# Two large transfers in place of eight small ones for the shifted copy of V in a local-attention layer

## The chip, the cores and the metric

The kernel runs on one core of a Trainium2 chip. The metric is device time in microseconds (us) of one execution. TensorE (PE in the rows) multiplies matrices, VectorE (DVE), ScalarE (ACT) and GpSimd (POOL) do the elementwise work, and SyncE (SP) issues the transfers, which 16 DMA engines carry out. Each engine works through its own list of instructions in order, and semaphores tie the lists together.

## The reference

A tensor of 2 x 1024 tokens with 128 channels goes through eight residual stages. Most of the time goes into a stage that comes twice, a stack of six layers with local attention. Cut to what matters here:

```python
def local_attention(q, k, v):              # 16 heads of 64, windows of w = 32 tokens
    bq, bk, bv = (t.reshape(b, h, n // w, w, d) for t in (q, k, v))
    def look(t):                           # the window before, and the window itself
        p = jnp.pad(t, ((0, 0), (0, 0), (1, 0), (0, 0), (0, 0)))
        return jnp.concatenate([p[:, :, :nw], p[:, :, 1:]], axis=3)
    bk2, bv2 = look(bk), look(bv)
    sim = jnp.einsum('bhwie,bhwje->bhwij', bq, bk2) * QK_SCALE
    ...
    attn = jax.nn.softmax(sim, -1)
    return jnp.einsum('bhwij,bhwje->bhwie', attn, bv2)

for i in range(DEPTH):                     # DEPTH = 6
    x = attn_layer(shift_tokens(x), Wqkv[i], q_scale[i], k_scale[i], Wo[i]) + x
    x = ffn_layer(shift_tokens(x), ln_g[i], ln_b[i], W1[i], b1[i], W2[i], b2[i]) + x
```

So each query looks at the 32 tokens of its own window and at the 32 before them.

## The kernel before

`window_layers` computes the six layers, and is called twice. Its work is cut into positions `(l, b, p)`: layer, batch, and pair of heads (8 pairs). Each engine has a function `position`, which writes out that engine's instructions of one position; layer 0 and the tail are written out, layers 1 to 5 are a hardware loop. In position `p`, a pair's queries and keys are made, while the scores, the maximum, the softmax and the values (`values`, L1470, and the sums of the weights, L1475) of the pair before, `p - 1`, are computed.

V is made for four heads, that is for two pairs, at once, in four tiles V0 to V3 of two 128-token units each (products L1530, evictions by ScalarE at L1685 into the tile `V[j % 2]`, 128 x 8 x 256 floats). The last of the four is made in an even position; in an odd one, the values begin to use it. Tokens lie on partitions, 128 to a unit, so that half of the 64 keys of a query block lie at another partition offset than V has them. For these there is a second tile, `V_early`, the same values 32 tokens later: partitions 32 to 127 hold V's partitions 0 to 95, and partitions 0 to 31 hold V's 96 to 127 of the unit before. The SP queue makes it by transfers from SBUF to SBUF (`shift`, L1315). `values` reads `V_early` and `V` in turn; in odd positions it first waits for the semaphore `v_moved`.

In an even position SP works in this order: `w_qk`'s load, when GpSimd has split the weights before them (`wqk_split`); `w_v`'s load (L1310), when GpSimd has split the `w_v` before (`wv_split`, whose second half is L1745); then the copies into `V_early`. Ahead of them stand a wait for the values that last read that buffer (`pv_full`) and waits for V's evictions (`taken_apart`). In the next, odd position SP first waits for TensorE's product Y1 (L1509), loads `w_o` (L1343), and goes on with `w_qk`.

Of the kernel before, what the change touches and what calls it, by code (L numbers as in the profile page):

```python
# [35 lines left out]
UNITS = N // 128  # L36
# [67 lines left out]
def build(nc, I, out):  # L104
# [42 lines left out]
    class Cut:  # L147
        at = size = 0
# [989 lines left out]
    def window_layers(last):  # L1138
# [4 lines left out]
        def own(name, shape, dt=F32):  # L1143
            return room.enter_context(nc.sbuf_tensor(f"{name}_{Room.uses}", shape, dt))
# [12 lines left out]
        V = [own(f"V{m}", [128, UNITS, 256]) for m in range(2)]  # L1157
        V_early = [own(f"V_early{m}", [128, UNITS, 256]) for m in range(2)]
# [67 lines left out]
        def numbered(l, places):  # L1226
            names = [(b, p, name) for b, p in places for name in fills_of(l, b, p)]
            return {name: n for n, name in enumerate(names)}

        PLACES = [(b, p) for b in range(B) for p in range(PAIRS)]  # L1230
        IN_FIRST, IN_LAYER, IN_TAIL = numbered(0, PLACES), numbered("any", PLACES), numbered(DEPTH, [(0, p) for p in range(7)])
# [20 lines left out]
        def need(eng, s, value):  # L1252
            if not (isinstance(value, int) and value <= 0):
                eng.wait_ge(s, value)
# [12 lines left out]
        def item(l, b, p):  # L1267
            return l * 16 + (8 * b + p)
# [6 lines left out]
        with stage("full", "free0", "free1", "free2", "free3", "max_full", "max_found", "max_turned", "rows_made", "wqk_in", "wqk_split", "wv_in", "wv_split", "wo_in", "scales_in", "tab_a_made", "tab_b_made",  # L1275
# [19 lines left out]
            def need_apart(eng, s, value):  # L1295

                need(eng, s, value)
                if not isinstance(value, int):
                    eng.sem_inc(passed, 1)

            def taken_apart(eng, l, b, p, name):
                need_apart(eng, free[bank_of(l, b, p, name)], before(l, b, p, name) + 1)

            @block.sync
            def _(sp):
                def qk_weights(layer, p):
                    sp.dma_start(w_qk[:, :], I["w_pairs"][bass.ds(layer * PAIRS + p, 1), :, 0:256].rearrange("o p n -> (o p) n")).then_inc(wqk_in, 16)

                def v_weights(layer, j):
                    sp.dma_start(w_v[:, :, :], I["w_pairs"][bass.ds(layer * PAIRS + 2 * j, 2), :, 256:384].rearrange("o p n -> p o n")).then_inc(wv_in, 16)  # L1310

                def shift(j, c):
                    for lo, hi, at in ((32, 128, 0), (0, 32, 1)):
                        first, end = 2 * c + at, min(2 * c + 2 + at, UNITS)
                        sp.dma_start(V_early[j % 2][lo:hi, first:end, :], V[j % 2][(lo + 96) % 128:(lo + 96) % 128 + hi - lo, first - at:end - at, :]).then_inc(v_moved, 16)  # L1315

                def scale_rows(layer):
                    for n, name in enumerate(("L1_ffn_q_scale", "L1_ffn_k_scale")):
                        src = I[name][bass.ds(layer, 1), :]
                        for dst, lo, at in ((scales, 0, 64 * n), (scales, 32, 64 * n + 32), (swapped, 32, 64 * n), (swapped, 0, 64 * n + 32)):  # L1320
                            sp.dma_start(dst[:, at:at + 32], src[:, lo:lo + 32].broadcast_to([128, 32])).then_inc(scales_in, 16)

                def ff_weights(layer):
                    sp.dma_start(w1[:, :], I["L1_ffn_W1"][bass.ds(layer, 1), :, :].rearrange("o p n -> (o p) n")).then_inc(ff_in, 16)
                    for n, (lo, width) in enumerate(FF):
                        sp.dma_start(w2[0:width, n, :], I["L1_ffn_W2"][bass.ds(layer, 1), lo:lo + width, :].rearrange("o p n -> (o p) n")).then_inc(ff_in, 16)
                    sp.dma_start(ff_cols[:, :], I["ff_cols"][bass.ds(layer, 1), :, :].rearrange("o p n -> (o p) n")).then_inc(ff_in, 16)
                    sp.dma_start(b2_row[:, :], I["L1_ffn_b2"][bass.ds(layer, 1), :].broadcast_to([128, C])).then_inc(ff_in, 16)

                def position(l, b, p):  # L1330
                    a, bb, oo, yy, ff = present(l, b, p)
                    it = item(l, b, p)
                    following = l if b == 0 or not a else (l + 1) % DEPTH if isinstance(l, int) else sp.snap((l + 1) % DEPTH)
                    if ff and p == 7 and b == 0:
                        taken_apart(sp, l, b, 6, "Z0")
                        taken_apart(sp, l, b, 6, "Z1")
                        ff_weights(l)
                    if a and p % 2 == 1:
                        if yy:
                            need_apart(sp, full, fill(l, b, p, "Y1") + 1)  # L1340
                        for m in range(2):
                            src = I["w_out_pairs"][bass.ds(l * PAIRS + (p - 1 + m), 1), :, :]
                            sp.dma_start(w_o[m][:, :], src.rearrange("o p n -> (o p) n")).then_inc(wo_in, 16)  # L1343
                    if ff and p == 1:
                        need(sp, staged_in, ff_index(l, b) * 2 + 2)
                        sp.dma_start(xs[1:113, 1, :, :], staged[0:112, :, :]).then_inc(xs_in, 16)
                        sp.dma_start(xs[113:128, 1, :, :], staged[112:127, :, :]).then_inc(xs_in, 16)
                        sp.dma_start(xs[0:1, 1, 1:BT, :], staged[127:128, 0:BT - 1, :]).then_inc(xs_in, 16)
                    if a:
                        if b == 1 and p == 1:  # L1350
                            need(sp, tab_a_made, l + 1)
                            need(sp, tab_b_made, l + 1)
                            scale_rows(following)
                        need_apart(sp, wqk_split, it * 2 + 4)
                        if p < 6:
                            qk_weights(l, p + 2)
                        else:
                            qk_weights(following, p - 6)
                        if p % 2 == 0:
                            j = p // 2  # L1360
                            need(sp, wv_split, ff_index(l, b) * 8 + (8 + 2 * j + 4))
                            if j < 2:
                                v_weights(l, j + 2)
                            else:
                                v_weights(following, j - 2)
                            need_apart(sp, pv_full, it - 2)
                            made_here = [c for c in range(4) if (b, p, f"V{c}") in IN_LAYER]
                            for c in range(4):
                                if c == 0 or c in made_here:
                                    taken_apart(sp, l, b, p, f"V{max(c, made_here[0])}")  # L1370
                                shift(j, c)

                qk_weights(0, 0)
                sp.dma_start(base_a[:, :, :], I["c_rot_a"].rearrange("p (t n) -> p t n", t=BT)).then_inc(bases_in, 16)
                sp.dma_start(base_b[:, :, :], I["c_rot_b"].rearrange("p (t n) -> p t n", t=BT)).then_inc(bases_in, 16)
                v_weights(0, 0)
                scale_rows(0)
                sp.dma_start(st_E, I["c_E"]).then_inc(loaded, 16)
                sp.dma_start(st_own, I["c_blocks"]).then_inc(loaded, 16)
                for u in range(2):  # L1380
                    sp.dma_start(st_other[64 * u:64 * u + 64, :], I["c_blocks"][64 - 64 * u:128 - 64 * u, :]).then_inc(loaded, 16)
                sp.dma_start(st_turn, I["c_turn"]).then_inc(loaded, 16)
                sp.wait_ge(wqk_split, 2)
                qk_weights(0, 1)
                sp.wait_ge(wv_split, 2)
                v_weights(0, 1)
                ff_weights(0)
                layers(sp, position, lambda: None)
                if last:
                    for b in range(B):  # L1390
                        sp.wait_ge(summed, 1 if b == 0 else 3)
                        sp.dma_start(out[b, :, :].rearrange("(t p) c -> p t c", p=128), x_tok[:, BT * b:BT * b + BT, :]).then_inc(stored, 16)
                    sp.wait_ge(stored, 32)

            @block.tensor
            def _(pe):
# [60 lines left out]
                def values(l, b, p, r):  # L1457
# [1 line left out]
                    need(pe, exp_done, r + 1)  # L1459
                    need(pe, o_done, r)  # L1460
                    if p % 2 == 1:
                        need(pe, v_moved, (r + 2) * 64)
                    if not isinstance(l, int):
                        pe.sem_inc(passed, 1)
                    for m in range(UNITS):
                        for t in range(2):
                            for w in range(2):
                                for h in range(2):
                                    rows, at, to = slice(64 * w, 64 * w + 64), 128 * (pair % 2) + 64 * h, 64 * m + QC * t
# [594 lines left out]
```

## Time and profile before

| | |
|---|---|
| median of 3 runs | 5618.77 us (5614.52 to 5621.3) |
| the profiled execution | 5640.73 us |
| its span, first to last instruction | 5638.9 us |
| TensorE busy, of the span | 85% |
| VectorE, ScalarE, GpSimd busy | 72%, 63%, 41% |
| mean granted TensorE clock | 0.933 |
| queue of SP's transfers, share of 16 engines | 11.0% |

The durations in the text are from the profiled execution; its time lies above the median of the runs. A share of busy time is a mean over stages, and says nothing by itself of what a change in one stage is worth.

### The profile page before, as it was taken

The numbers are of one execution on the slowest core, as the hardware profiler recorded it, in microseconds if no ns is written. First come the engines' busy times: TensorE is split into PE (matmuls) and PEld (weight loads), VectorE is DVE, ScalarE is ACT, GpSimd is POOL, SyncE is SP. The second block draws the span as 40 slices with busy tenths as digits, with TensorE's granted clock in tenths as the row PEclk, the third lists the DMA queues.
The fourth block names the chain that finished last, engine by engine and source line by source line (L and its number), as shares of the span: only waits on it lengthen the run. The fifth ranks groups of instructions, "written<-read, shape, count | busy, mean of one in ns | idle before, by whom it ended". The sixth has DMA issues, their size and how long they took to land. (4 is left out here: it accounts for less than half of the span.)

```text
span 5638.9 us, 214849 instructions
## 1 busy us (share of the span) xinstructions
PE 4803.0 (85%) x90306; PEld 3553.2 (63%) x90306; DVE 4084.8 (72%) x6116; ACT 3578.6 (63%) x5848; POOL 2338.4 (41%) x2473
## 2 busy tenths in 40 slices
PE   8997996788888888888887899788888888888887
PEld 3333432577777777777776333577777777777776
DVE  7885654677777777777775788677777777777775
ACT  5784664466666666666665577666666666666664
POOL 1100100365455555455553110465545555555552
PEclk8997997899999999999998899899999999999998
DMA  0000000111111111111110000111111111111111
GB/s 13 2 2 6 2 2 10 46 48 39 42 46 40 44 47 44 37 45 46 39 53 26 5 2 2 47 49 44 45 38 43 48 38 46 42 44 40 46 45 33
DMA packets 191142, 188.14 MB, mean 33 GB/s; under 512 B 45716, under 2 KB 138160, under 8 KB 190104
## 3 DMA queue, kind: packets, MB, share of 16 engines
q1 hardware_dynamic: 190104, 173.61, 11.0%
q8 instruction: 736, 12.06, 0.9%
q14 instruction: 302, 2.47, 0.1%
HBM read 68.26 MB, written 1.05 MB: 12 GB/s over the span
## 5 line engine op out<-in xcount | busy, mean ns | idle before, releaser
L1761 POOL TENSOR_TENSOR cross<-raw,tab_b 128x512 f32<-128x512 f32 x768 | 995.0, 1327 | 121.2 <-ACT raw L1634 115.0
L740 DVE TENSOR_REDUCE arena<-PS 128x1 f32<-128x512 f32 (+3 forms) x1408 | 828.8, 647 | 221.4 <-PE PS L553 135.7
L1767 POOL CAST kT_b<-kT 128x512 bf16<-128x512 f32 x384 | 239.8, 624 | 1583.0 <-ACT kT L1687 1583.0
L691 ACT ACTIVATE arena<-PS 128x1024 f32<-128x1024 f32 (+1 forms) x704 | 669.2, 968 | 203.5 <-PE PS L576 128.3
L1849 DVE TENSOR_TENSOR rot<-PS,tab_a 128x512 f32<-128x512 f32 x768 | 498.6, 684 | 275.8 <-ACT raw L1634 234.0
L1872 DVE TENSOR_TENSOR rot<-rot,inv_norm 128x1024 f32<-128x1024 f32 x384 | 532.1, 1386 | 191.7 <-ACT inv_norm L1650 182.0
L1663 ACT ACTIVATE log_den<-PS 128x1024 f32<-128x1024 f32 x192 | 197.2, 1027 | 599.0 <-PE PS L1475 599.0
L1634 ACT COPY raw<-PS 128x512 f32<-128x512 f32 x768 | 440.4, 596 | 213.5 <-PE PS L1493 182.0
L1493 PE MATMUL PS<-w_qk_high,x_high 128*128 128x256 f32 x1536 | 475.1, 309 | 109.9 <-ACT kT L1687 66.2
L1865 DVE TENSOR_TENSOR rot<-rot,cross 128x1024 f32<-128x1024 f32 x384 | 533.9, 1390 | 8.7 <-POOL cross L1761 8.0
L1538 PEld LDWEIGHTS PS<-ident,rot 128*128 128x128 f32 x3072 | 357.6, 148 | 276.1 <-issue 201.3
L1440 PE MATMUL PS<-qT,kT 64*64 64x32 f32 x24576 | 447.3, 226 | 97.8 <-issue 97.6
L553 PE MATMUL PS<-k_parts,q_parts 32*128 32x512 f32 (+3 forms) x1408 | 476.2, 510 | 42.3 <-ACT arena L673 27.0
L1538 PE MATMUL PS<-ident,rot 128*128 128x128 f32 x3072 | 432.3, 289 | 73.5 <-DVE rot L1872 37.2
L1440 PEld LDWEIGHTS PS<-qT,kT 64*64 64x64 f32 x24576 | 420.8, 142 | 108.2 <-issue 108.1
L1640 ACT ACTIVATE squares<-raw 128x1024 f32<-128x1024 f32 x384 | 406.8, 1059 | 128.2 <-DVE norms L1858 109.0
L1858 DVE TENSOR_REDUCE norms<-squares 128x16 f32<-128x1024 f32 x384 | 466.4, 1215 | 0.4 <-ACT squares L1640 0.4
L1470 PE MATMUL PS<-PT,V_early 64*64 64x32 f32 x12288 | 420.5, 229 | 47.8 <-issue 37.3
L553 PEld LDWEIGHTS PS<-k_parts,q_parts 32*128 32x128 f32 x1408 | 218.6, 194 | 375.8 <-issue 324.1
L1876 DVE TENSOR_TENSOR oT<-PS,rec_den 128x1024 f32<-128x1024 f32 x192 | 234.5, 1222 | 303.0 <-ACT rec_den L1666 302.7
L1470 PE MATMUL PS<-PT,V 64*64 64x32 f32 x12288 | 420.4, 228 | 38.2 <-issue 37.7
L605 PE MATMUL PS<-arena 128*32 128x256 f32 (+1 forms) x5376 | 432.8, 394 | 8.2 <-issue 3.9
(259 smaller groups left out, 11965.0 us busy)
## 6 DMA issues: line engine op xcount, KB each, us to landing
V_early<-V SPq DMA_DIRECT2D x384, 192.0 KB
w_qk<-in_w_pairs SPq DMA_DIRECT2D x196, 128.0 KB, 2.2
V_early<-V SPq DMA_DIRECT2D x288, 64.0 KB
w_v<-in_w_pairs SPq DMA_DIRECT2D x100, 128.0 KB, 2.2
w_o<-in_w_out_pairs SPq DMA_DIRECT2D x192, 64.0 KB, 2.1
xs<-staged SPq DMA_DIRECT2D x24, 224.0 KB, 2.5
w<-in_L_ffn_W SPq DMA_DIRECT2D x12, 341.0 KB
q_parts<-max_rows SPq DMA_DIRECT2D x192, 2.0 KB
```

What stands on the lines that cost most here:

```text
L553: last = nc.tensor.matmul(bank[:, 0:keys], q[r, 128 * qt:128 * qt + 128], k[r, 512 * kh:512 * kh + keys], start=True, stop=not masked, til ...
L691: nc.scalar.activation(PT[u % 6].rearrange("p (a n) -> p a n", a=2)[:, :, first_q:512], PS[:, 2 * (u % 2):2 * (u % 2) + 2, first_q:512], A ...
L740: nc.vector.tensor_reduce(maxima[:, 2 * m + h, qt, kh:kh + 1], bank[:, 0:keys_of(qt, kh)], AX.X, ALU.max).then_inc(bank_free, 1)
L1440: last = nc.tensor.matmul(PS[64 * w:64 * w + 64, 4 + h, 64 * m + QC * t:64 * m + QC * t + QC], kT[par][rows, at:at + 64], qT[par][rows, at ...
L1470: nc.tensor.matmul(PS[64 * h:64 * h + 64, 6 + w, to:to + QC], (V_early, V)[t][pair // 2 % 2][rows, m, at:at + 64], PT[rows, h, to:to + QC] ...
L1493: last = nc.tensor.matmul(bank[:, 256 * j:256 * j + 256], x_parts[b][m][:, PAD + 128 * t:PAD + 128 * t + 128], wqk_parts[w][:, :], start=n ...
L1538: last = nc.tensor.transpose(bank[:, 128 * j:128 * j + 128], rot[:, 4 * f + j, lo:lo + 128], ident[:, :])
L1761: nc.gpsimd.tensor_tensor(dst[:, :, :, o:o + 32], src[:, :, :, other:other + 32], tab[:, :, o:o + 32].unsqueeze(2).broadcast_to([128, 8, 2 ...
L1849: nc.vector.tensor_tensor(rot[:, 2 * i:2 * i + 2, :].rearrange("p t (w h d) -> p (t w) h d", w=2, h=2), bank.rearrange("p (c h d) -> p c h ...
L1858: nc.vector.tensor_reduce(norms2[h][:, :], squares[:, :].rearrange("p (c d) -> p c d", d=64), AX.X, ALU.add).then_inc(red_done, 1)
L1865: nc.vector.tensor_tensor(d, d, cross[h][:, :], ALU.add).then_inc(add_done, 1)
L1872: nc.vector.tensor_tensor(d, d, inv_norm[h][:, :].unsqueeze(2).broadcast_to([128, 16, 64]), ALU.mult).then_inc(rot_done, 1)
```

## The change

`shift` goes. In an even position SP waits for V3's eviction and for the values of that very position (`pv_full` at `it`, not at `it - 2`), and issues two transfers that copy all eight units: 96 partitions with rows of 8 KB, and 32 partitions with rows of 7 KB. Before, there were four pairs, one for each tile of two units, 192 KB and 64 KB (32 KB for the last), each behind the eviction of its tile where that falls into the position. The count that `values` waits for is adapted.

```diff
-                def shift(j, c):
-                    for lo, hi, at in ((32, 128, 0), (0, 32, 1)):
-                        first, end = 2 * c + at, min(2 * c + 2 + at, UNITS)
-                        sp.dma_start(V_early[j % 2][lo:hi, first:end, :], V[j % 2][(lo + 96) % 128:(lo + 96) % 128 + hi - lo, first - at:end - at, :]).then_inc(v_moved, 16)
-
...
-                            need_apart(sp, pv_full, it - 2)
-                            made_here = [c for c in range(4) if (b, p, f"V{c}") in IN_LAYER]
-                            for c in range(4):
-                                if c == 0 or c in made_here:
-                                    taken_apart(sp, l, b, p, f"V{max(c, made_here[0])}")
-                                shift(j, c)
+                            taken_apart(sp, l, b, p, "V3")
+                            need_apart(sp, pv_full, it)
+                            sp.dma_start(V_early[j % 2][32:128, :, :], V[j % 2][0:96, :, :]).then_inc(v_moved, 16)
+                            sp.dma_start(V_early[j % 2][0:32, 1:UNITS, :], V[j % 2][96:128, 0:UNITS - 1, :]).then_inc(v_moved, 16)
...
-                        need(pe, v_moved, (r + 2) * 64)
+                        need(pe, v_moved, (r + 2) * 16)
```

## Rows read from the trace of the kernel before

**Rows 1.** The page: the span, and the chain that ended last.
```profile
span 5638.9 us, 214849 instructions
...
PE 20%; ACT 7%; issue 6%; DVE 3%; ACTq 0%; POOL 0%; SPq 0%; DMA 0%; DVEq 0%; POOLq 0%
```

**Rows 2.** The SP queue's waits: us in total, times, longest us.
```profile
SPq L1310 <- POOL w_v_low L1745: 1183.8, 96, 18.2
...
SPq L1299 <- PE PS L1509: 277.5, 80, 6.6
```

**Rows 3.** The timeline around one set of copies: start us, us, engine, what.
```profile
2008.88 0.59 ACT L1685 COPY V<-PS 128x512 f32<-128x512 f32 x1 [0.52 <-PE PS L1530]
...
2013.49 1.96 PE L1475 MATMUL PS<-PT,ones 64*64 64x512 f32 x8
...
2023.01 0.73 POOL L1745 TENSOR_TENSOR w_v_low<-w_v,w_v_high 128x256 fp32r<-128x256 f32 x1
...
2024.56 5.00 SPq L1315 DMA_DIRECT2D V_early<-V  x8
...
2036.07 0.32 PE L1470 MATMUL PS<-PT,V_early 64*64 64x32 f32 x8
```

**Rows 4.** The tile V_early: issues (ns min/median/max), and waits (us, times).
```profile
L1315 SPq DMA_DIRECT2D V_early<-V x768: 516/589/2180, 1070.9 to 5564.8; - x192
...
  DMA V_early<-V: 2.2, 3
```

**Rows 5.** The timeline of a short position, with the longest of these waits.
```profile
1180.71 6.16 SPq L1315 DMA_DIRECT2D V_early<-V  x8
...
1189.83 0.32 PE L1470 MATMUL PS<-PT,V_early 64*64 64x32 f32 x8 [1.76 <-DMA V_early<-V]
```

**Rows 6.** Two loads at the stage's start: issues, then size and us to landing.
```profile
1036.03 0.43 SPq L1374 DMA_DIRECT2D base_a<-in_c_rot_a  x1
1036.51 0.42 SPq L1375 DMA_DIRECT2D base_b<-in_c_rot_b  x1
...
base_b<-in_c_rot_b SPq DMA_DIRECT2D x1, 512.0 KB, 5.5
```

**Rows 7.** Stretches of the copies of rows 3; the last columns are PEclk, DMA share, GB/s.
```profile
2024.50:2025.50 1.00, 1.00 (x43) 0.73 (x41) 0.66 (x1) 0.81 (x2) 0.00 (x0) 1.00 0.37 112
2025.50:2027.50 2.00, 1.71 (x24) 1.48 (x12) 1.98 (x5) 1.83 (x3) 1.91 (x2) 1.00 0.73 200
2027.50:2029.50 2.00, 1.34 (x11) 1.26 (x12) 2.00 (x4) 0.83 (x3) 2.00 (x3) 1.00 0.68 203
2029.50:2031.00 1.50, 1.50 (x41) 1.33 (x43) 1.50 (x3) 1.36 (x4) 1.50 (x2) 1.00 0.59 163
```

**Rows 8.** Loads of instructions, DMA view of 4010.5:4012, 2109.2:2110.5, 5011:5013: packets, MB, share.
```profile
q8 instruction: 1, 0.02, 4.2%
...
q8 instruction: 1, 0.02, 4.4%
...
q8 instruction: 1, 0.02, 5.6%
```

**Rows 9.** TensorE's waits: us in total, times, longest us.
```profile
PE PS L1440 <- issue: 97.6, 99, 3.5
```

**Rows 10.** TensorE's timeline: scores during copies, without copies, and behind two stops.
```profile
5011.41 1.83 PE L1440 MATMUL PS<-qT,kT 64*64 64x32 f32 x112
5014.18 0.43 PE L1440 MATMUL PS<-qT,kT 64*64 64x32 f32 x16 [0.95 <-issue]
...
5032.47 2.06 PE L1440 MATMUL PS<-qT,kT 64*64 64x32 f32 x128
...
4949.08 0.66 PE L1440 MATMUL PS<-qT,kT 64*64 64x32 f32 x30 [1.39 <-issue]
```

**Rows 11.** Stretches around the stop at 4949.08, columns as in rows 7.
```profile
4946.00:4950.50 4.50, 3.11 (x158) 2.89 (x145) 4.47 (x5) 2.92 (x6) 3.81 (x4) 1.00 0.02 4
4950.50:4961.00 10.50, 9.30 (x155) 7.45 (x153) 6.19 (x20) 4.85 (x11) 0.56 (x2) 0.51 0.05 16
```

## The prediction

> **What bounds the kernel now.** I read the page first. One core spends 5638.9 us, and the chain that ended last runs mostly through TensorE's own work, with a share called "issue", time in which TensorE waited for nothing that the profile shows [rows 1]. No DMA has a visible share of that chain. So the first question is whether the copies of V are anywhere in the way.
>
> I then read what the SP queue waits for, since it issues the copies. Two rows matter. Ahead of the copies stands the load of w_v, which waits for GpSimd's split of the previous w_v (1183.8 us over 96 times); behind them stands the load of w_o, which waits for TensorE's product L1509 (277.5 us over 80 times, 3.5 us each) [rows 2]. The timeline of one even position shows the order [rows 3]. V's last tile is evicted at 2008.88 to 2009.47. The position's values end with L1475 at 2015.45. GpSimd's split of w_v, its last work of the position, ends at 2023.74. Only then does SP issue w_v's load, and the eight copies follow at 2024.56. So already now the copies begin some 9 us behind the values of their position. They are read by the values of the next position, at 2036.07, 11.5 us after the first issue.
>
> The rows of the tile V_early say how often that is too late: three waits, 2.2 us in the whole run [rows 4]. The longest, 1.76 us, is in a short position: first copy at 1180.71, values at 1189.83 instead of 1188.07 [rows 5]. So the need comes 7.4 us after the first issue in that short position, 11.5 in the long one.
>
> **The change, part by part.**
>
> *The waits on SP.* The wait for V3 and the wait for the values of the position (`pv_full` at `it` in place of `it - 2`) stand behind the wait for w_v's split, which ends 8.3 us after the values and 14 us after V3's eviction [rows 3]. Both are met when SP arrives. Cost: 0. The cover is the split; without it SP would stop until the values end, and behind it in the queue would be only w_o, which waits for a later product anyway. TensorE's changed count (two transfers of 16 per even position, so `(r + 2) * 16`) asks for the same copies and costs no instruction.
>
> *Issuing two transfers for eight.* An issue has a median of 589 ns [rows 4]. Six fewer are 3.5 us of SP per even position, 96 times. What hides them: SP then waits for L1509, 3.5 us on average today [rows 2], and it will wait longer. Gain on the path: 0. w_o is neither earlier nor later.
>
> *Landing.* The same bytes are moved: 96 rows of 8 KB and 32 rows of 7 KB, 992 KB, in place of four pairs with rows of 2 KB (1 KB at the end). Today the eight issues take 5.0 to 6.2 us [rows 3, 5], and their rate sets the pace: the DMA engines are 0.37 to 0.73 busy meanwhile [rows 7]. The nearest row for the new form is the start of the stage: two loads of 512 KB, issued 0.48 us apart, the second landing 5.5 us after its issue, 6.0 us after the first [rows 6]. At 1024 KB that is slightly more than 992 KB, though from HBM, with rows of 4 KB. As a lower bound I squeeze today's traffic to a share of 1.00: 1.0 x 0.37 + 2.0 x 0.73 + 2.0 x 0.68 + 1.5 x 0.59 = 4.1 us [rows 7], and about 1 us more for start and end (an estimate: the first copy's issue stands 1 us before the share rises over 0.37): 5. So 5 to 6 us after the first issue, against some 9 in the short position now [rows 5]. Both ends are before 7.4, the earliest need. So the waits go: **-2.2 us**, and the other 93 passages gain nothing, since nobody waited there.
>
> *What the denser transfer meets.* The one thing that the copies can disturb is other traffic. The engines' own work isn't slowed by it: 112 score products took 1.83 us during copies, 128 took 2.06 us without, 16 ns each in both [rows 10]. What shares the DMA engines is the loading of TensorE's instructions, 16 KB at a time. One such load took 4.2% of 16 engines in 1.5 us where nothing else moved, so 0.042 x 16 x 1.5 = 1.01 us; during copies one took 4.4% in 1.3 us, so 0.92 us, and another 5.6% in 2 us, so 1.79 us [rows 8]. So a load meets from 0 to some 0.8 us of delay today. TensorE feels it: the scores of the position after an even one stop in the middle for 0.95 us at 5014.18, for no wait that the profile names, just after that long load [rows 8, 10]. Over the run L1440 has 99 such stops, 97.6 us [rows 9]. I put half of them, about 50, at the odd positions, where the copies move (an estimate; the scores are the same in both). In the new form the load meets a DMA share near 1.0 instead of some 0.65 for a shorter time. Bounds for one stop: the delay vanishes (-0.8, if the copy is out of the way) or each load is doubled (+1.0, a load alone taking 1.01). The mean delay today lies near the low end of 0 to 0.8, since one of two sampled loads shows none; I take 0.2, half as much again for the half as dense again share, so +0.1 us on 50 stops: **+5 us**. Ends: -2.2 to +46 us without more.
>
> A rule of the Trainium skill speaks against large rows here. "DMA: Bandwidth & Descriptors", section on queues, rings and completion order, says that an engine goes round its queues and drains a whole packet from one before it turns to the next. By that rule an instruction load would stand behind 8 KB pieces instead of 2 KB ones, and the delay would grow with the piece, not with the share; the time by it is the second rival's. No row of this trace shows an instruction load behind a piece over 4 KB.
>
> *Sum.* -2.2 + 5 + 0 + 0 = +2.8 us on the profiled execution's 5640.7 us: 5643.5. The median of the runs shown, 5618.77, is 22 us below the profiled execution; I carry the difference over unchanged: 5618.8 + 2.8, about 5621 us.
>
> **The rivals.**
>
> *1. The forecast: nothing that can be measured.* 0.2% of 5618.77 is 11 us, which is about what a measurement of this kernel can tell from no change; -2.2 and +5 lie inside it. For it speaks that only three of 96 passages waited for the copy.
>
> *2. Slower: instruction loads behind the dense copy.* Place: the scores of the odd positions, 2 to 6 us after the first copy. If each of the 50 stops grows by 0.3 us, it is 15 - 2.2 = +13 us, 5632; by 0.6, 30 - 2.2 = +28, 5647. It decides from (11 + 2.2)/50 = 0.26 us per stop. There is a second step: longer stops can cost clock. A stop of 1.39 us at 4949.08 [rows 10] was followed by a stretch with a granted clock of 0.51 for 10.5 us, after 1.00 before it [rows 11]; 0.51 is the lower level, 1.2 GHz. The stop of 0.95 us had none behind it. Ten more such stretches at up to 5 us each would be up to +50 us. For it: the 1.79 us load. Against: the copy is over 3 us sooner, and one of the two loads sampled during copies met no delay [rows 8].
>
> *3. Faster: the copy gets out of the way.* If the copy is over by 5 us, the loads that start later are free again. At most the 0.8 us of delay goes from perhaps 15 of the 50 stops: -12 us, -14 with the waits, 5605. Against: the loads before a stop at 5.7 us, as at 5014.18, start some 3 us after the first issue, inside the new transfer.
>
> *4. Slower: the large transfers land late.* If rows of 8 KB were moved at half the rate of the 4 KB ones, the landing would come at 9 to 10 us. Then short positions wait up to 2.6 us; with a third of 96 passages short and 1.3 us in the mean, +42 us, 5660. It decides from 7.4 us. Against: 1024 KB landed in 6.0 us [rows 6].
>
> That the change does not do all that it says is part of the forecast: the copies are behind the values already, and only their number and density change.
>
> **How the numbers follow.** Forecast 0.64, second rival 0.19, third 0.12, fourth 0.05. Faster by over 0.2% takes the third: 0.12; slower the second and fourth: 0.24; within 0.2%: 0.64. The likeliest gives 5621 us, its own range 5608 to 5630. The whole range goes from 5606, where the third rival's ends, to 5648, the second at 0.6 us per stop, and leaves out some clock stretches and the fourth: 5606 to 5648.
>
> **What would show it.** In the changed kernel's trace: two issues on SP right behind w_v's load, some 9 us after L1475, both within 1.3 us (right: waits cost nothing); no wait of L1470 on V_early (right: landing); a DMA share near 1.0 for 3 to 4 us after the first issue. L1440's stops on "issue": near 98 us in 99 times if the fetch term is small, 115 or more if rival 2 holds, below 85 if rival 3 does. The wait of w_o's load for L1509 should grow from 3.5 to about 7 us each. The prediction is wrong if L1470 waits for V_early, or if more or fewer stretches of half clock stand in the odd positions.

## The result and the profile after

The changed kernel takes 5794.9 us (median of 4 runs, 5786.94 to 5806.86), against 5618.51 us before: 1.0307 times as long, 95% interval 1.0289 to 1.0325. The forecast was 5621 us, no change, with a range to 5648. It was wrong, and by far. Behind the change line numbers are 7 lower: the scores L1440 are L1433, the values L1470 are L1463, L1509 is L1502, L1530 is L1523 (L1343 is 5 lower, L1338). The copies stand at L1363 and L1364.

The page of the changed kernel, span and chain, answers to [rows 1]:

```profile
span 5785.5 us, 214035 instructions
...
PE 21%; ACT 7%; issue 6%; DVE 3%; ACTq 0%; POOL 0%; DVEq 0%; DMA 0%; SPq 0%; POOLq 0%
...
V_early<-V SPq DMA_DIRECT2D x96, 768.0 KB, 5.6
...
V_early<-V SPq DMA_DIRECT2D x96, 224.0 KB, 6.0
```

The chain's shares are as before, and no DMA stands among them: they tell nothing of where 147 us of span went. The last two lines give the copies' time to landing, 5.6 us for the large one and 6.0 us, from an issue 0.6 us later, for the other.

SP's waits answer to [rows 2]:

```profile
SPq L1310 <- POOL w_v_low L1738: 1157.6, 96, 18.0
...
SPq L1299 <- PE PS L1502: 812.4, 80, 14.0
```

The copies are still behind w_v's split, as forecast. SP then waits 10.2 us for L1502, up from 3.5 us: the time that it saves at issuing, and the time that TensorE comes later.

TensorE's waits (us in total, times, longest us), answering to [rows 9]; the row on top is the scores:

```profile
PE PS L1433 <- issue: 218.8, 108, 4.0
...
PE PS L1463 <- issue: 47.9, 57, 2.3
...
PE PS L1523 <- issue: 28.9, 18, 3.2
...
PE PS L1486 <- issue: 21.4, 6, 3.8
...
PE PS L1468 <- issue: 6.2, 11, 1.2
```

The same view of the kernel before, for the lines that answer to the lower four:

```profile
PE PS L1470 <- issue: 75.1, 67, 3.7
...
PE PS L1493 <- issue: 25.4, 7, 3.8
PE PS L1530 <- issue: 18.8, 17, 3.8
...
PE PS L1475 <- issue: 4.3, 9, 0.9
```

Before, the five sum to 221.2 us with the 97.6 of [rows 9]; after, to 323.2. So 102 us of the loss is time in which TensorE stood with no wait that the profile names, and it is in the scores: they stop for 121 us more, the other four for 19 us less. No row of L1463 waits for V_early any more.

Counted by place in the trace, the scores' stops that begin within 9 us of a position's first copy went from 56 with 37.9 us (the longest 1.20) to 63 with 151.8 us (the longest 3.97); all others from 43 with 59.7 us to 45 with 67.0. So they grew where the copies move, and hardly elsewhere.

One odd position shows it. TensorE's and SP's timeline of the changed kernel:

```profile
2141.95 0.55 SPq L1363 DMA_DIRECT2D V_early<-V  x1
2142.55 0.59 SPq L1364 DMA_DIRECT2D V_early<-V  x1
...
2144.89 0.78 PE L1433 MATMUL PS<-qT,kT 64*64 64x32 f32 x40
2148.55 2.57 PE L1433 MATMUL PS<-qT,kT 64*64 64x32 f32 x88 [2.88 <-issue]
```

The DMA view of the same kernel in two windows, 2142 to 2145.5 and 2145.5 to 2147.5 (packets, MB, share of 16 engines):

```profile
q1 hardware_dynamic: 351, 0.78, 85.0%
...
q1 hardware_dynamic: 75, 0.35, 65.0%
q8 instruction: 1, 0.02, 3.7%
```

And stretches of it (busy time of PE, PEld, DVE, ACT, POOL, then PEclk, DMA share, GB/s), answering to [rows 7, 11]:

```profile
2143.00:2145.50 2.50, 2.50 (x88) 2.38 (x87) 2.50 (x4) 1.78 (x5) 2.50 (x3) 1.00 1.03 264
2145.50:2147.00 1.50, 0.17 (x12) 0.09 (x6) 1.50 (x3) 0.19 (x1) 1.50 (x2) 1.00 0.84 232
2147.00:2148.50 1.50, 0.00 (x0) 0.00 (x0) 1.50 (x2) 0.00 (x0) 1.50 (x2) 0.72 0.12 30
2148.50:2152.00 3.50, 3.45 (x92) 3.38 (x92) 3.50 (x5) 0.82 (x1) 2.25 (x3) 0.50 0.02 5
```

The reader is to see four things. The copy fills the DMA engines (a share of 1.03; it sums the times of packets by where they begin, so it can pass 1). In its first 3 us no load of TensorE's instructions is moved; one comes only in the second window, and once it moves it takes 3.7% of 32 us, 1.18 us, inside the 0.92 to 1.79 us of [rows 8]. TensorE stops at 2145.7 and stands for 2.88 us, where before the stops at this place lasted 1.20 us at most, like the 0.95 us of [rows 10]. And behind the stop the granted clock is 0.50, 1.2 GHz: the 88 score products that follow take 2.57 us, 29 ns each, against 16 ns in [rows 10].

That such a stop waits for a load is seen over the whole trace. A load of 16 KB comes every 8 us or so (736 in the span), yet of TensorE's 156 unnamed stops of over 0.8 us in the changed kernel eight in ten end 1.26 to 1.56 us behind the end of such a load, and one alone under 1.2 us; of the 112 in the kernel before eight in ten end 1.28 to 1.54 us behind it.

The parts add up. 102 us is stops, and 4 us is waits of TensorE that the profile names (582 us before, 586 after). The trace's records of the granted clock sum to 762 us at half clock before and 844 after; 82 us more at half clock lose some 41 us (an estimate that takes TensorE as the pace there). 102 + 4 + 41 = 147, and the spans differ by 146.6 us. Within 20 us behind a position's first copy the time at half clock went from 29 to 230 us; elsewhere it fell from 733 to 614, and no run here shows why. (The medians differ by 176 us, as the profiled execution of before stands 22 us above its median and that of after 8 us below.)

The trace records when each load of instructions begins to move. Over the 96 sets of copies, counted from the issue of the first copy of a set:

```
loads that begin          0 to 3.5 us   3.5 to 6 us   behind the first issue
before                        48            40
changed                        3            79
```

### The profile page after: what moved, and what is told of

It reads as the page before. It is cut to its first block and busy times, and to the rows that moved or that the text cites. A ratio compares the mean times of both kernels' runs of the same rounds, so it can differ in the third digit from the quotient of the medians.

```text
span 5785.5 us, 214035 instructions
## 1 busy us (share of the span) xinstructions
PE 4844.6 (84%) x90306; PEld 3603.3 (62%) x90306; DVE 4088.2 (71%) x6116; ACT 3582.5 (62%) x5848; POOL 2345.7 (41%) x2473
## 5 line engine op out<-in xcount | busy, mean ns | idle before, releaser
L1433 PE MATMUL PS<-qT,kT 64*64 64x32 f32 x24576 | 455.4, 226 | 219.4 <-issue 218.8
L1433 PEld LDWEIGHTS PS<-qT,kT 64*64 64x64 f32 x24576 | 426.4, 143 | 231.6 <-issue 231.3
L1463 PE MATMUL PS<-PT,V 64*64 64x32 f32 x12288 | 408.1, 224 | 42.1 <-issue 41.4
L1652 ACT ACTIVATE PT<-PS 128x1024 f32<-128x1024 f32 x192 | 197.1, 1026 | 394.1 <-PE PS L1433 393.7
L1486 PE MATMUL PS<-w_qk_low,x_high 128*128 128x256 f32 x1536 | 439.0, 286 | 0.0
```

The source lines that it names most:

```text
L1433: last = nc.tensor.matmul(PS[64 * w:64 * w + 64, 4 + h, 64 * m + QC * t:64 * m + QC * t + QC], kT[par][rows, at:at + 64], qT[par][rows, at ...
L1463: nc.tensor.matmul(PS[64 * h:64 * h + 64, 6 + w, to:to + QC], (V_early, V)[t][pair // 2 % 2][rows, m, at:at + 64], PT[rows, h, to:to + QC] ...
L1486: last = nc.tensor.matmul(bank[:, 256 * j:256 * j + 256], x_parts[b][m][:, PAD + 128 * t:PAD + 128 * t + 128], wqk_parts[w][:, :], start=n ...
```

## The experiments

Three theories. A: a load stands behind a few pieces of the copy, so that the delay goes with the size of a piece, as the second rival has it. B: a load stands behind all that the transfers have queued. C: TensorE's list is shorter in the loop ((r + 2) * 16 costs fewer instructions than (r + 2) * 64; the traces count 4520 instructions of its sequencer against 4560, some 4 a pass of the loop where the expectations say 8), so that the cuts between its loads fall elsewhere. Ratios are to the kernel before on the same chip, with 95% intervals.

**Pieces of 1 KB.**

```diff
-V_early = [own(f"V_early{m}", [128, UNITS, 256]) for m in range(2)]
+V_early = [own(f"V_early{m}", [128, UNITS, 264])[:, :, 0:256] for m in range(2)]
```

> The changed kernel with the units of V_early 264 floats apart instead of 256, so that its two transfers are cut into pieces of 1 KB and not 8 KB; same bytes, same two issues, same count on TensorE. Theory A (a load of instructions stands behind a few pieces of the copy, so the delay goes with the size of a piece): 1 KB pieces delay it less than the 2 KB ones of the kernel before; 5600 to 5640 us. Theory B (a load stands behind all that the transfers have queued, whatever the pieces): the queue is as long as in the changed kernel, 5780 to 5820 us. Theory C (TensorE's list of instructions is 8 shorter in the loop, so that the cuts between its loads fall elsewhere): the list is that of the changed kernel, so 5780 to 5810 us too.

Measured: 5781.42 us, 1.0277 (1.0247 to 1.0306). Nearly all of the loss stays with pieces of an eighth of the size, smaller than the 2 KB ones of before. Scores stop for 210.4 us in 120 times. Theory A, by the size of a piece, falls.

**Two pairs of transfers.**

```diff
-sp.dma_start(V_early[j % 2][32:128, :, :], V[j % 2][0:96, :, :]).then_inc(v_moved, 16)
...
+for c in range(2):
+    sp.dma_start(V_early[j % 2][32:128, 4 * c:4 * c + 4, :], V[j % 2][0:96, 4 * c:4 * c + 4, :]).then_inc(v_moved, 16)
+    end = min(4 * c + 5, UNITS)
+    sp.dma_start(V_early[j % 2][0:32, 4 * c + 1:end, :], V[j % 2][96:128, 4 * c:end - 1, :]).then_inc(v_moved, 16)
...
-need(pe, v_moved, (r + 2) * 16)
+need(pe, v_moved, (r + 2) * 32)
```

> The changed kernel with two pairs of transfers (four units each, rows of 4 KB) in place of one pair. Theory A (piece size): between the two kernels, about 5660 to 5720 us. Theory B (all that is queued): four issues take 2.4 us, the bytes some 3.5 us, so the queue never runs empty until the end; the first transfers alone queue half as much, but the rest arrives before they end: 5740 to 5800 us. Theory C (cuts of TensorE's list): 5780 to 5810 us if the list is that of the changed kernel, 5615 if it is that of before.

Measured: 5675.22 us, 1.0101 (1.0071 to 1.013), where theory A had put it and lower than B's figure. TensorE's list has the length of before here (4560), and there is a loss, so C alone does not explain it. With the run above, this points to how much one transfer queues at once, not to the size of its pieces: 38 loads begin 2.5 to 3.5 us behind the first issue, about when the first transfer is over (a first piece some 1.2 us after the issue, and six pieces of 4 KB at 0.235 us). B as I wrote it, which let the second pair hold the loads too, was too strict.

**The late waits alone.** The changed kernel's two waits, with the four pairs of before behind them.

```diff
 taken_apart(sp, l, b, p, "V3")
 need_apart(sp, pv_full, it)
-sp.dma_start(V_early[j % 2][32:128, :, :], V[j % 2][0:96, :, :]).then_inc(v_moved, 16)
...
+for c in range(4):
+    sp.dma_start(V_early[j % 2][32:128, 2 * c:2 * c + 2, :], V[j % 2][0:96, 2 * c:2 * c + 2, :]).then_inc(v_moved, 16)
...
```

> One part of the change alone: the waits for V3 and for the values of the position, with the four pairs of transfers of the kernel before. All theories that put the loss on the transfers (A, B) expect the time of before, 5615 to 5625 us, since both waits are met when SP arrives. A theory that puts it on the waits expects 5750 us or more.

Measured: 5622.31 us, 0.9995 (0.9977 to 1.0013). The waits cost nothing that this run shows; the loss comes with the two large transfers in place of eight.

**No copies.**

```diff
-sp.dma_start(V_early[j % 2][32:128, :, :], V[j % 2][0:96, :, :]).then_inc(v_moved, 16)
...
-need(pe, v_moved, (r + 2) * 16)
...
-(V_early, V)[t][pair // 2 % 2][rows, m, at:at + 64]
+(V, V)[t][pair // 2 % 2][rows, m, at:at + 64]
```

> No copies at all: V_early is not written, and the values read V in its place (so the attention over the window before is computed with other values), with no wait for them. It shows what the copies cost in either kernel. Theories A and B: the loads of instructions in the odd positions meet nothing; if the delay in the kernel before is some 0.2 us on 50 stops and the three waits of 2.2 us go, 5595 to 5610 us; then the eight small transfers cost 10 to 25 us and the two large ones 185 to 200.

Measured: 5567.95 us, 0.9908 (0.988 to 0.9935). The eight small transfers of the kernel before cost 5621.8 - 5568.0 = 54 us on that chip, more than the 10 to 25 expected. So the kernel before already paid for its copies, and not through the three named waits of 2.2 us. Nor did it pay in the scores, where the prediction looked: they stop as long without copies (103.7 us in 96 times, against 97.6 in 99). It is the values, L1470 before and L1457 here:

```profile
PE PS L1457 <- issue: 43.4, 48, 2.2
```

They stopped for 75.1 us before. The rest is in the products of V (18.8 to 8.5 us) and in the time at half clock (762 to 694 us), in one profile of each.

**The same list for TensorE.** Both transfers count 64, and TensorE waits for (r + 2) * 64 as before.

```diff
-... .then_inc(v_moved, 16)
+... .then_inc(v_moved, 64)
-need(pe, v_moved, (r + 2) * 16)
+need(pe, v_moved, (r + 2) * 64)
```

> The changed kernel, but each of its two transfers counts 64 instead of 16, so that TensorE waits for (r + 2) * 64 as before: its list of instructions then has the length of the kernel before (8 register instructions more in the loop than the changed one). Theory C (the cuts of the list moved): back to about 5620 us. Theory B (a load of instructions stands behind all that the transfers have queued): 5780 to 5810 us as the changed kernel. In between, 5690 to 5750: both have a share.

Measured: 5793.53 us, 1.033 (1.0294 to 1.0367). The list has the length of before (4560), and nothing is gained. Theory C falls.

**One of the two transfers.**

```diff
-sp.dma_start(V_early[j % 2][0:32, 1:UNITS, :], V[j % 2][96:128, 0:UNITS - 1, :]).then_inc(v_moved, 16)
...
-need(pe, v_moved, (r + 2) * 16)
+need(pe, v_moved, (r + 2) * 8)
...
```

> The changed kernel with the large transfer of 96 partitions alone; the one of 32 partitions is left out (those rows of V_early stay zero). Theory B: a load of instructions stands behind what is queued, and the queue of each DMA engine is shorter by its two pieces of 7 KB, 0.43 us each in the changed kernel's trace, so 0.85 us. Some 50 stops shorter by 0.85 us are 43 us, and fewer stretches at half clock some 10 to 30 more: 5715 to 5750 us, as against 5795. If the loss goes with the size of a piece alone (theory A), the 8 KB pieces are still there: 5780 us or more.

Measured: 5727.35 us, 1.0193 (1.0173 to 1.0213). A queue 0.85 us shorter takes 68 us off, in the range of theory B and below that of A. The scores' row of TensorE's waits in this run:

```profile
PE PS L1432 <- issue: 186.6, 109, 4.0
```

It is 32 us below that of the changed kernel, where 43 were expected. The 10 to 30 us more by the clock do not show in the profile: the time at half clock is 868 us, against 844. The loads cluster at the end of the single transfer: 51 of them begin 4.0 to 4.5 us behind its issue.

**The two large transfers sooner.** Ahead of w_v's load in SP's order, where the wait for the values now binds.

```diff
+taken_apart(sp, l, b, p, "V3")
+need_apart(sp, pv_full, it)
+sp.dma_start(V_early[j % 2][32:128, :, :], V[j % 2][0:96, :, :]).then_inc(v_moved, 16)
+sp.dma_start(V_early[j % 2][0:32, 1:UNITS, :], V[j % 2][96:128, 0:UNITS - 1, :]).then_inc(v_moved, 16)
 need(sp, wv_split, ff_index(l, b) * 8 + (8 + 2 * j + 4))
 ...
-taken_apart(sp, l, b, p, "V3")
-need_apart(sp, pv_full, it)
...
```

> The two large transfers ahead of the load of w_v in SP's order instead of behind it, so that they start when the values of the position end, some 8 us sooner, and are over when the next position begins. Theory B: the loss depends on whether TensorE needs a load of instructions in those 5 us. In the trace of before, 54 loads start 2 to 4 us behind the first copy as it stands now, and 25 to 35 in the stretch from 8 to 2 us ahead of it, so about half the loss: 5660 to 5720 us. A theory by which large transfers cost the same wherever they stand expects 5780 us or more.

Measured: 5573.1 us, 0.9934 (0.9913 to 0.9955): faster than both kernels, and better than the 5660 to 5720 us expected. (The expectation's 25 to 35 loads in the stretch ahead do not come out of the trace of before, which has 57 from 8 to 2 us ahead of the first copy.) The same transfers that lost 3% gain 0.7% when they start some 7 us sooner: the first copy's issue comes 0.1 us behind the last L1468 in place of 7.5 us (medians). Two rows of this run tell why: a stretch of the copy, and the scores' waits.

```profile
2042.00:2044.50 2.50, 1.72 (x15) 1.48 (x14) 1.23 (x1) 2.50 (x5) 0.87 (x2) 1.00 0.99 256
```

```profile
PE PS L1433 <- issue: 93.3, 90, 4.6
```

The copy fills the DMA engines just as much (0.99), but here TensorE works on transposes and on query and key products of 256 columns, 15 instructions in 2.5 us, where the changed kernel issued 88 in 2.5 us. Few loads stand in that stretch (11 begin in the first 3.5 us), and the scores' stops are below even those of [rows 9]. All of TensorE's unnamed stops sum to 187 us here, 189 without copies, 229 in the kernel before and 330 in the changed one.

**The four small pairs as V's tiles are made**, ahead of w_v's load, in the kernel before.

```diff
+need_apart(sp, pv_full, it - 2)
+for c in range(4):
+    ...
+    shift(j, c)
 need(sp, wv_split, ff_index(l, b) * 8 + (8 + 2 * j + 4))
 ...
```

> The kernel before with its four pairs of transfers ahead of the load of w_v instead of behind it: they then really start as V's tiles are made, during the scores and values of the even position. Theory B: the short queues of 192 KB and 64 KB delay a load by at most some 0.7 us, but the scores and values are where most loads are needed: 5615 to 5660 us. If loads are not delayed by short transfers at all, the three waits for the copies go and it is 5610 to 5620.

Measured: 5596.8 us, 0.9975 (0.9963 to 0.9987). A small gain, below both ranges expected: the loss by theory B did not come, though the copies now start during the scores and values of the even position. The scores stop for 89.5 us, the values for 60.9, less than the 97.6 and 75.1 of before.

**Place against size: the small pairs behind the values, and the large ones once more.** The first is the run above with `pv_full` at `it` and all four pairs behind V3; the second repeats the large ones unchanged.

> The four pairs of small transfers at the place of the two early large ones: behind the values of the position, ahead of w_v's load. It parts place from size. Theory B: where no stop stands, size counts for nothing: 5570 to 5590 us, like the two large ones there. If it is the large size that pays there, it should be like the pairs made early, 5597 us or more.

> The two early large transfers once more, on the same chip as the small ones at that place and with more rounds: 0.9934 of the kernel before in the first run, so 0.992 to 0.995 again.

Measured on one chip: the small pairs 5593.97 us, 0.9956 (0.994 to 0.9972); the large ones 5590.48 us, 0.995 (0.9933 to 0.9966). At this place the size makes no difference that these runs show, though the first median lies 4 us above its 5570 to 5590 us, and the second ratio at the edge of its 0.992 to 0.995. What pays is the order, not the size of the transfers.

## Why the prediction was wrong

*The waits on SP: right.* Cost 0, shown by the late waits alone, 0.9995.

*Issuing two for eight: right.* No gain; SP's wait for L1502 rose from 3.5 to 10.2 us where I had said about 7; TensorE is later too.

*Landing: right.* 5.6 us for the large transfer, and 0.6 + 6.0 = 6.6 us after the first issue for the second, against 5 to 6 forecast and 7.4 needed. The waits of 2.2 us went. That a short position would still need the copies at 7.4 us was not put to the test, as TensorE came later.

*"What the denser transfer meets" is the step that failed.* I priced a load's delay by the share of the DMA engines: 0.2 us today, half as much again for a share half as dense again, +0.1 us on 50 stops, +5 us; the upper bound was a load that takes twice as long, +46 us (50 stops at 1.0 us, less the 2.2, are 48). It measured +102 us in stops and some 41 us at half clock. The number of stops was right, 56 in the odd positions; each grew by some 2 us, not by 0.1. The load is not slowed, it is held back: once it moves it takes 1.11 us in the median in both kernels, but behind 96 first copies 3 loads begin in the first 3.5 us where 48 did. The rows that I sampled could not show that: each tells how long a load moved [rows 8], none when TensorE began to want it. The upper bound should have been the whole copy, not one load.

*The second rival* had the right place, its sign came true (115 us of the scores' stops or more; 218.8 measured), and its second step, the clock, was right. But its price was too small, 0.3 to 0.6 us per stop, and so was its chance of 0.19. Beside it stood a rule of the Trainium skill, "DMA: Bandwidth & Descriptors", section on queues, rings and completion order, by which an engine turns to another queue only after a whole packet. I took one piece, which the profile's rows count as a packet, for one packet of that rule. So read, it does not agree with the runs: pieces of 1 KB hold the loads nearly as long as pieces of 8 KB (1.0277 against 1.0307). But that section of the Trainium skill gives a packet about 9 to 17 descriptors, and a descriptor one contiguous run, so that the large transfer's six pieces on an engine could be one packet (an estimate from that figure). A load would then stand behind the whole transfer, as the 51 loads at the end of the single one do. So the runs speak against my reading of the rule, and not against the rule; what a packet is here, no run shows.

*The third rival* took the end of the copy at 5 us as a gain; the loads of the scores are wanted before that. *The fourth* did not happen.

*What bounds the kernel:* I read three waits of 2.2 us as all that the copies cost, with a small delay in the scores. Without copies the kernel before is 54 us faster, and not in the scores.

Open: by what rule a DMA engine orders a load and a copy. The trace does not name the engine of a packet. That a load waits for the transfers that were queued before it was wanted fits the large transfers, the two pairs and the single transfer; with pieces of 1 KB 23 loads begin 2.5 to 3.5 us behind the first issue, in the middle of the transfer, which it does not explain.

## What to carry to other kernels

Transfers of a kernel share the DMA engines with the loads of its own instructions, and here a large SBUF copy held most of these back until a transfer was nearly over. An "issue" wait in the middle of many small matmuls is the row to look at. To bound its price, take the whole copy's length (6.6 us to landing here, with stops of up to 4.0 us), and add what the half clock costs that can follow such a stop. Try a large copy beside instructions that are few and long: moving it by 7 us here was worth 3.5%, and its size alone cost 3% in one place and nothing that these runs show in another. To learn what a hidden transfer costs, run the kernel without it.

## What was not expected of the hardware

A copy from SBUF to SBUF of 768 KB in 96 rows kept nearly every 16 KB load of instructions from beginning in the first 3.5 us after its issue (3 loads began there, 48 with the small transfers). TensorE went on some 1.4 us after such a load was in. The 8 KB pieces took 0.50 us each in the mean, those of 2 KB 0.113 us, so that large pieces moved no faster: 16.4 against 18.1 GB per second and engine.
